# Heads stage of a frequency-attention kernel: the 128x128 channel mix of one chunk at a time becomes a mix of two chunks on the four 64x64 quarters of the array

## What is computed

```python
xf = jnp.fft.fft2(x)
qf = xf.reshape(b, HEADS, hd, h * w)                       # 8 heads of 16 channels
attn_f = jax.lax.complex(softmax(attn_f.real), softmax(attn_f.imag))
out_cplx = jnp.einsum('bhcd,bhdn->bhcn', attn_f, qf)
out_f = jnp.abs(jnp.fft.ifft2(out_cplx)).reshape(b, c, h, w)
...
fsa = _conv(jnp.concatenate([out_f, out_f_l], axis=1), projf_w)
```

## Time and profile before

| | us |
|---|---|
| median of three runs | 24949.8 |
| the profiled execution's own time | 24943.67 |
| its span | 24941.9 |
| heads stage of the first image, from its first row copy to its last root | 528.9 to 703.6 |
| output stage of the first image | about 1281 to 1660 |
| layer 1 | from about 11400 to the end |

### The profile page before, as it was taken

The page is one execution under the profiler, slowest core; times in us unless marked ns, Lnnn a source line. Parts: engine busy times, 40 slices in busy tenths (PEclk is TensorE's granted clock), DMA queues, the critical chain, the costliest instruction groups (busy, mean ns, idle before and its releaser), DMA issues.

```text
span 24941.9 us, 329327 instructions
## 1 busy us (share of the span) xinstructions
PE 22557.0 (90%) x107489; PEld 13255.3 (53%) x107489; DVE 19918.5 (80%) x23961; ACT 13275.5 (53%) x18807; POOL 12339.5 (49%) x4613
## 2 busy tenths in 40 slices
PE   5999999999999999998888888888888888888888
PEld 4777778687777777684333333333333333333333
DVE  4666657465666657468999999999999999999999
ACT  2323141323223131325777777777777777777776
POOL 0000000000000000005999999999999999999998
PEclk8999999999999999999999999999999999999999
DMA  3122221303022221304444444444444444444444
GB/s 98 42 88 74 80 82 42 120 22 107 35 91 70 81 81 46 102 25 153 168 167 189 167 192 168 168 191 168 166 190 166 187 173 168 191 167 166 191 166 165
DMA packets 866693, 3187.54 MB, mean 128 GB/s; under 512 B 68265, under 2 KB 340026, under 8 KB 579770
## 3 DMA queue, kind: packets, MB, share of 16 engines
q1 hardware_dynamic: 866234, 3181.65, 34.6%
HBM read 2884.91 MB, written 296.49 MB: 128 GB/s over the span
## 4 chain that ended last, share of the span: by engine, by line
PE 33%; DVE 9%; issue 6%; ACT 4%; DMA 2%; DVEq 0%; ACTq 0%; POOL 0%; SPq 0%; POOLq 0%
PE yp L2051 16%; PE pj L2007 8%; DVE hid L2274 4%; DVE hid L2280 3%; PE pj L2036 2%; PE pj L2066 2%; PE pj L2024 2%; PE pj L2015 2%; PE yp L2043 1%; ACT t L2133 1%; DMA img<-x 1%; DVE delta L2316 1%; DMA bc<-bc_rows 1%; ACT xn L2147 1%; ACT du L2181 1%
## 5 line engine op out<-in xcount | busy, mean ns | idle before, releaser
L2382 POOL TENSOR_TENSOR hid<-hid,bc 128x2048 f32<-128x2048 f32 x2048 | 7814.9, 3816 | 908.2 <-DVE carry L2288 905.6
L2051 PE MATMUL yp<-hid,ident 128*128 128x512 f32 x16384 | 7346.5, 597 | 428.2 <-POOL hid L2382 428.2
L2356 POOL TENSOR_SCALAR_AFFINE_SELECT ident<-ident 128x128 f32<-128x128 f32 x1 | 0.3, 295 | 11436.1 <-DVE ident L2241 11436.1
L2051 PEld LDWEIGHTS yp<-hid,ident 128*128 128x128 f32 x16384 | 3040.8, 189 | 4626.9 <-issue 3960.4
L2274 DVE TENSOR_TENSOR_SCAN hid<-da,carry,t 128x512 f32<-128x512 f32 x3968 | 4857.3, 1266 | 111.0 <-DVE carry L2288 9.7
L2280 DVE TENSOR_TENSOR_SCAN hid<-t,carry,hid 128x512 f32<-128x512 f32 x3968 | 4827.8, 1258 | 29.9 <-ACT t L2122 29.4
L2375 POOL TENSOR_TENSOR hid<-bc,du 128x1024 f32<-128x1024 f32 x2048 | 4102.0, 2003 | 196.7 <-PE yp L2051 170.5
L2122 ACT ACTIVATE t<-delta,v_a 128x512 f32<-128x512 f32 x4096 | 2660.1, 681 | 1574.0 <-DVE hid L2280 1571.0
L1202 PE MATMUL bk<-region 128*128 128x256 f16 (+2 forms) x30640 | 3379.4, 266 | 61.3 <-ACT region L1559 43.7
L2007 PE MATMUL pj<-xn,w_x 128*128 128x512 f32 x4096 | 2373.3, 733 | 1077.8 <-ACT xn L2147 1030.0
L1202 PE MATMUL bk<-work,region 128*128 128x256 f16 x27336 | 3164.8, 274 | 23.6 <-DVE region L1047 20.5
(11 more groups left out here) (288 smaller groups left out, 22499.4 us busy)
## 6 DMA issues: line engine op xcount, KB each, us to landing
bc<-bc_rows SPq DMA_DIRECT2D x1024, 2048.0 KB, 7.2
work<-in_shift_d SPq DMA_DIRECT2D x256, 512.0 KB, 3.8
work<-in_x SPq DMA_DIRECT2D x256, 256.0 KB, 2.7
work<-in_x SPq DMA_DIRECT2D x128, 512.0 KB, 5.1
xpad<-in_x SPq DMA_DIRECT2D x32, 2048.0 KB, 12.4
gated<-work SPq DMA_DIRECT2D x256, 256.0 KB, 2.4
region<-gated SPq DMA_DIRECT2D x256, 256.0 KB, 2.9
region<-heads SPq DMA_DIRECT2D x256, 256.0 KB, 3.1
```

The source lines that it names most:

```text
L2051: m = nc.tensor.matmul(yp[:, h, :], ident[:, :], hid[:, k % 4, n, :], start=False, stop=(g == G - 1 and n == 3), skip_group_check=True)
L2382: nc.gpsimd.tensor_tensor(hid[:, k % 4, :, :], hid[:, k % 4, :, :], bc[:, g, 1, :, :], ALU.mult).then_inc(s_hc.sem, 1)
```

## The change

The stage now walks pairs m = 0..15. A pair has two chunks: rows 4m..4m+3 and rows 64+4m..64+4m+3 (`place(m, blk)` = m + 16 blk). Their split parts are kept until both are there, in four `shifted` buffers. The mix of a pair is then made in two halves, o = 0 (real) and o = 1 (imaginary), one in each chunk body. A half has 24 matmuls of 64x64 weights by 512 columns, in groups of four. The four of a group take the two halves r of the channels (rows of the array) and the two chunks blk (columns of the array). Bank 3 + 2o + r then holds channel half r, with chunk m on partitions 0 to 63 and chunk m + 16 on 64 to 127. A pair so needs four squares, two sums and two roots, as many as two chunks did.

```diff
-        shifted = [... for i in range(2)]
+        shifted = [... for o in (1024, 3072, 6144, 4096)]
-        sq2 = [wk(2048 + 512 * i, 512) for i in range(2)]
+        sq2 = [wk(o, 512) for o in (2048, 2560, 10624, 11136)]
-        OF = region[:, 0:HW].rearrange("p (a h) -> p a h", h=P)
+        OF = region[:, 0:HW].rearrange("p (r a h) -> p r a h", r=2, h=64)
...
+        NM = NK // 2
+        place = lambda m, blk: m + NM * blk
+        def heads_loop(eng, body):
+            body(0, 0)
+            body(1, 1)
+            with eng.Fori(1, NM // 2 - 1) as i:
+                body(i * 2, 0)
+                body(i * 2 + 1, 1)
+            body(NM - 2, 0)
+            body(NM - 1, 1)
...
 vector:
+                def add_squares(m):
+                    for r in range(2):
+                        dve.wait_ge(s_os.sem, s_os.at(b, 4 * m + 3 + r))
+                        V.tensor_tensor(sq2[r], sq2[r], sq2[2 + r], ALU.add).then_inc(s_oa.sem, 1)
+                def body(m, mp):
+                    for blk in range(2):
+                        n_ = 2 * m + blk
...
+                        if not (isinstance(n_, int) and n_ == NK - 1):
+                            turned_rows(n_ + 1)
+                        if blk == 0 and not (isinstance(m, int) and m < 2):
+                            add_squares(m - 2)
+                        if more:
+                            next_rows(b + 1, n_, blk)
...
 sync, output stage:
-                    sp.dma_start(of[par], of_d[0:1, :, bass.ds(kk * 512, 512)]...).then_inc(sof[par], 16)
+                    for r in range(2):
+                        for blk in range(2):
+                            part = of[par].rearrange("p (a h w) -> p a h w", a=4, h=2)[64 * r:64 * r + 64, :, blk, :]
+                            sp.dma_start(part, of_d[0:1, 64 * blk:64 * blk + 64, bass.ds(kk * 256 + r * 8192, 256)].rearrange("a c (j w) -> (a c) j w", w=64)).then_inc(sof[par], 16)
...
 tensor:
+                def mix(m, mp, o):
+                    if o == 0:
+                        pe.wait_ge(s_shr.sem, s_shr.at(b, 2 * m + 2))
+                        pe.wait_ge(s_shi.sem, s_shi.at(b, 2 * m + 2))
+                    pe.wait_ge(s_os.sem, s_os.at(b, 4 * m - 2 + 2 * o))
+                    pe.sem_inc(s_mix.sem, 1)
+                    for n_, (w_, part) in enumerate((((0, 0), (2, 1)), ((0, 1), (1, 0)))[o]):
+                        for wh, ph in ((0, 0), (0, 1), (1, 0)):
+                            for r in range(2):
+                                rows_ = slice(64 * r, 64 * r + 64)
+                                for blk in range(2):
+                                    x_ = mm(bk[3 + 2 * o + r][64 * blk:64 * blk + 64, :], mix16[rows_, w_, wh, rows_], shifted[2 * mp + blk][rows_, part, ph, :], ...)
+                    x_.then_inc(s_o.sem, 1)
...
 scalar:
+                def squares(m, o):
+                    act.wait_ge(s_o.sem, s_o.at(b, 2 * m + 1 + o))
+                    if o == 0:
+                        act.wait_ge(s_of.sem, s_of.at(b, 2 * m))
+                    else:
+                        act.wait_ge(s_oa.sem, s_oa.at(b, 2 * m))
+                    for r in range(2):
+                        cp(sq2[2 * o + r], bk[3 + 2 * o + r][:, :], ACT.Square, ...).then_inc(s_os.sem, 1)
+                def root(m):
+                    for r in range(2):
+                        act.wait_ge(s_oa.sem, s_oa.at(b, 2 * m + r + 1))
+                        cp(OF[:, r, :, bass.ds(m * 4, 4)], sq2[r].rearrange("p (j a) -> p a j", j=4), ACT.Sqrt).then_inc(s_of.sem, 1)
+                def body(m, mp):
+                    for blk in range(2):
+                        n_ = 2 * m + blk
+                        if not (isinstance(n_, int) and n_ == NK - 1):
+                            take_rows(n_ + 1, place(m, 1) if blk == 0 else place(m + 1, 0))
...
+                        act.wait_ge(s_sh.sem, s_sh.at(b, n_ + 1))
+                        act.wait_ge(s_o.sem, s_o.at(b, 2 * m - 2))
+                        cp(shifted[2 * mp + blk][:, 0, 0], bk[1][:, :], scale=HSCALE).then_inc(s_shr.sem, 1)
+                        if blk == 0 and not (isinstance(m, int) and m < 2):
+                            root(m - 2)
+                        if not (isinstance(m, int) and m == 0):
+                            squares(m - 1, blk)
```

More of the change, by code:

```diff
@@ L1368, in turn @@
                     m.then_inc(s_tr.sem, 1)
[L1370 to L1376, removed]
-                        for n_, (w_, part) in enumerate(terms):
-                            for wh, ph in ((0, 0), (0, 1), (1, 0)):
-                                m = mm(o, mix16[:, w_, wh, :], shifted[par][:, part, ph, :], start=(n_ == 0 and wh == 0 and ph == 0), stop=(n_ == 1 and wh == 1))
-                    m.then_inc(s_o.sem, 1)
@@ new lines, in body @@
+                def body(m, mp):
+                    for blk in range(2):
+                        n_ = 2 * m + blk
+                        pe.wait_ge(s_trc.sem, s_trc.at(b, n_ + 1))
+                        pe.wait_ge(s_kl[blk], b * (8 * NK) + m * 16 + 16)
+                        pe.wait_ge(s_shr.sem, s_shr.at(b, n_))
+                        pe.wait_ge(s_shi.sem, s_shi.at(b, n_))
+                        for j in range(4):
+                            for s in range(2):
+                                x_ = mm(bk[1 + s][:, j * P:(j + 1) * P], turned[:, j * P:(j + 1) * P], kbuf3[blk][:, j, s * P:(s + 1) * P], start=True, stop=True)
+                        x_.then_inc(s_sh.sem, 1)
+                        if not (isinstance(n_, int) and n_ == NK - 1):
+                            turn(n_ + 1)
+                        if not (isinstance(m, int) and m == 0):
+                            mix(m - 1, 1 - mp, blk)
@@ L1397, in image @@
                 pe.wait_ge(s_abs.sem, s_abs.at(b, NK))
                 turn(0)
-                rows_loop(pe, body)
-                mix(NK - 1, 1)
+                heads_loop(pe, body)
+                mix(NM - 1, 1, 0)
+                mix(NM - 1, 1, 1)
                 pe.wait_ge(s_os.sem, s_os.at(b, 2 * NK))
@@ L1654, in body @@
-                def body(kk, par):
-                    if not (isinstance(kk, int) and kk < 3):
-                        root(kk - 3)
-                    if not (isinstance(kk, int) and kk == NK - 1):
-                        take_rows(kk + 1)
-                    act.wait_ge(s_sh.sem, s_sh.at(b, kk + 1))
-                    act.wait_ge(s_o.sem, s_o.at(b, kk - 1))
-                    cp(shifted[par][:, 0, 0], bk[1][:, :], scale=HSCALE).then_inc(s_shr.sem, 1)
-                    if not (isinstance(kk, int) and kk < 2):
-                        squares(kk - 2, par)
@@ L1665, in image @@
-                take_rows(0)
-                rows_loop(act, body, 2)
-                root(NK - 3)
-                for kk in range(NK - 2, NK):
-                    squares(kk, kk % 2)
-                    root(kk)
+                def squares(m, o):
[5 more added lines that the diff above has]
+                    for r in range(2):
+                        cp(sq2[2 * o + r], bk[3 + 2 * o + r][:, :], ACT.Square, scale=1.0 / (HSCALE * HWEIGHT)).then_inc(s_os.sem, 1)
@@ L1672, in points_high @@
+                take_rows(0, 0)
+                heads_loop(act, body)
+                root(NM - 2)
+                squares(NM - 1, 0)
+                squares(NM - 1, 1)
+                root(NM - 1)
                 def points_high(ready, high, j, buf, tiles=slice(0, 4)):
```

89 lines of the change are left out of this document (34 added, 55 removed).

## The result

The changed kernel takes **25355.2 us** (median of 4 runs, 25349.95 to 25357.92) against 24948.5 us (median of 4 runs beside it): ratio **1.0163**, 95% interval 1.0145 to 1.018. It is 407 us slower; the profiled executions differ by 414 us in their spans (25356.1 against 24941.9), 51.8 us for each of the eight images.

What follows compares the result with a forecast made beforehand. It saw the heads stage bound by PE's work (5.06 us per chunk) and a nearly equal PE-DVE loop without the mix (4.81). Chain 19.9, tail 1.7, loads 8.9, clock 10: 40.5 us per image, 324 in eight, 25268 us; range 25120 to 25460.

Steps and rivals of the forecast that it cites:

- The chain, 19.9 us: Heads stage: ACT's roots wait for DVE sums of the same body, delaying the next copy; +19.9 us per image.
- the long interval: Heads stage: second of a pair's two intervals between DVE's first splits, 6.94 us beside 4.81; thirteen of 31 are long.
- The loads, 8.9: Heads loop on ACT: two table loads in each of six turns, 1.5 us per turn, +8.9 us per image.
- the clock, 10: Heads stage: PE's idle gaps in long intervals bring its clock to half speed behind them; some +10 us per image.
- Six long gaps and half of seven: Heads stage: PE gaps counted as losing clock, six with a load and half of seven shorter, 1.3 us each.
- My price of 1.28 us in the chain: Heads stage: a table load behind the first root's wait adds 1.28 us, without the skill page's 2.66 us.
- The tail, 1.7: End of heads stage, last chunk's first split to last root: from 9.7 to about 11.4 us, +1.7 per image.
- The output stage, 0: Load of heads as four DMAs issued 0.52 us apart, the last 1.6 us later, still in time: 0 us.
- PE's wait for `heads`: Output stage: sign of being wrong; the forecast expected no PE wait for the heads loads.
- My rival for it: Output stage: heads loads land late, PE waits 0.6 to 2.5 us every second chunk, 77 to 320 us; chance 0.09.
- PE-bound relief: Heads stage: rival that PE was the bound, all intervals fall to 4.81 us, -49 us, 24895 us; chance 0.05.
- quarters not side by side: Heads stage mix: rival that quarter matmuls run singly (25640 us) or two abreast (25360 us); chance 0.06 together.

Runs made afterwards that it cites:

- e12: The changed kernel with ScalarE's heads loop peeled by one more pair of bodies (no table loads in the loop) and eight extra filling matmuls on TensorE: 25190.0 us.
- e1: The changed kernel with ScalarE's heads loop peeled by one more pair of bodies, so no table loads stand in the loop: 25247.2 us.
- e7: The changed kernel with TensorE's wait for the turned rows moved to last of the four waits ahead of the shift: 25333.3 us.
- e8: e5 with TensorE's wait for the turned rows moved to last of the four waits ahead of the shift: 24895.9 us, ratio 0.9979.
- e3: e1 with ScalarE's order changed, the roots moved to a pair's second half body and the squares rearranged: 24960.9 us, ratio 1.0005.
- e2: The changed kernel, table loads kept, with eight extra matmuls filling TensorE's longest idle time: 25286.8 us.
- e5: e3 with the load of heads as two DMAs of 1 KB pieces and its reading matmul split in two: 24910.2 us, ratio 0.9985.
- e4a: The kernel before with only the output stage's load of heads split into four DMAs of 256-byte pieces: 24989.1 us, ratio 1.0017.

## Why the prediction was right, and where it was off

The forecast was 25268 us, the range 25120 to 25460; it is 25355: slower by 407 us where I had 324. Point by point, per image:

- **The chain, 19.9 us for 31 intervals.** Shown. e12 has it without loads and at full clock: 181.1 - 156.9 = 24.2 us, up to 1.3 of which are the extra matmuls themselves (the first four intervals of an image take 21.7 us there and 20.4 in e1). What was too small is the long interval: forecast at 6.94, thirteen times 7.27 on average in e12, 4.2 us in all. The other eighteen add up to the forecast's 86.6 us, though the short ones are 4.64 and not 4.81. Step by step in the pair shown: L901 starts at 7.48 (forecast 7.55), L883 1.21 later as forecast, but from there to the next L899 it is 3.26 us and not 2.99, so the pair takes 11.95 and not 11.75. I took that last step from a short interval of the kernel before, where PE is hardly ever idle. Behind a long idle time the waits in a row make it longer, which e7 and e8 show by another order of them (1.07 to 0.73 us). That e7 then has 6.95 beside my 6.94 is partly chance, since its short interval isn't the forecast's. e3 removes the chain and with it the loss.
- **The loads, 8.9, and the clock, 10: together 18.9.** Measured together: 200.7 - 181.1 = 19.6. That the sum comes so near is partly luck. Six long gaps and half of seven at 1.3 us are 12.4, and I had written 10. A fall of the clock was dearer behind a load than forecast (intervals of 10.4 us and more against 8.56, 1.9 us; 35 of 48) and cheaper and rarer without one (8.2 against 7.32, 0.9 us; 15 of 56, where I had counted half). By parts, filling the changed kernel gives 8.3 of clock, which leaves 11.3 for the loads, and these contain the low clock that filling couldn't prevent; six loads in the chain at 1.24 are 7.4. My price of 1.28 us in the chain stands (1.24 in e2). Here, not the 2.66 us of the Trainium skill ("ScalarE: Activation LUTs", What ACT_TABLE_LOAD costs), was the right source. The clock's mechanism was right. Which gaps bring it down is open: the length of the idle time doesn't tell them apart.
- **The tail, 1.7.** From the last L899 to the end of the last root it went from 9.65 to 11.8 us, mean of eight images: +2.2. No experiment has it alone. e3 and e5 still have it (11.6 us), though their chain is gone.
- **The output stage, 0.** This is the step that failed, and one of the prediction's own signs of being wrong, PE's wait for `heads`, appeared. It is +3.5 us per image, 28 us in all, and e4a shows it in the kernel before. I had put the four issues at 0.52 us from one to the next, from the earlier trace rows, rows of DMAs with one piece per partition; these take 0.60 to 0.63 and come 0.79 apart. So the last is issued 2.4 us later and not 1.6. I priced the pieces on the DMA engines, and the landing wasn't slow: 64 KB in 256-byte pieces land in 2.4 us. The Trainium skill ("DMA: Bandwidth & Descriptors", Specifications) warns that pieces under 512 bytes don't reach line rate. In these runs the landing shows nothing of it, and the engines' time only the small rise given under e4a and e4b. The cost lay in SP's queue, a place the forecast had counted at the old price. My rival for it gave 77 to 320 us on the condition that a load lands over 3.1 us after its issue. That condition didn't come true; the wait came from the issues, and its size was 28.
- **The rest.** About 2.3 us per image lie outside these terms: 0.9 between the last root and the output stage, 1.4 elsewhere. For e3 the heads stage, the tail and the output stage add up to +2 us and +11 were measured; for e5 it is -34 and -39. I didn't trace these, and they stay open.

Terms as measured: 43.8 + 2.2 + 3.5 + 2.3 = 51.8 us against 40.5, times eight 414 against 324. Of the rivals, PE-bound relief is refuted by the even intervals that never came, and quarters not side by side by 24 matmuls in 1.49 us.

## What to carry to other kernels

When an engine's instruction waits for something made in the same body, and another engine's next step is queued behind it, the loop becomes that chain, however idle all engines are; move the waiting instruction half a body later before you give up the rest of the change. Here that one move turned a kernel 1.2% slower into one that is level, with the cheaper mix still in it (e1 to e3). Price a table load, an idle time or a DMA issue by where it stands (0, 0.44 or 1.24 us for the same load), and price the issue of a DMA from a row of the same form, in partitions and in pieces.

## What the runs showed of the hardware that I had not expected

- The same idle time of 2.41 us on TensorE was followed by matmuls at full speed (0.66 us for four) and at half (1.12 us) in one image of one kernel. Eight extra matmuls in it made the kernel 57 us faster.
- The issue of a DMA on SP took 0.33 us for 32 or 128 pieces of 2 KB, one per partition, and about 0.62 us for 128 pieces of 1 KB or 256 of 256 bytes on 64 partitions. But 512 pieces of 512 bytes on 128 partitions took 0.37 us and 64 of 12 bytes on 64 partitions 0.59, so the number of pieces doesn't set it.
- TensorE works off waits one after another, about 0.1 us for each that comes behind the one it was held at (in the changed kernel's trace the records of these waits begin at 2084.86, 2085.00 and 2085.10, after the copy's end at 2084.82): 1.07 against 0.73 us from the copy's start to the matmul in long intervals, by order alone. Reordering wasn't free in the short ones: 0.74 became 0.82.
- Whether two table loads stand in each turn of a hardware loop depended on how many bodies were written out ahead of it: one pair of bodies more on ScalarE and twelve loads per image became one.
